# A two-layer decoder: head scores from spread keys in 32-row tiles instead of from zero-padded keys by head

## What is computed

```python
Q, K, V = (a.reshape(B, S, 16, 8).transpose(0, 2, 1, 3) for a in (x @ wq.T, c @ wk.T, c @ wv.T))
score = jnp.einsum('bhqd,bhkd->bhqk', Q, K) / jnp.sqrt(8)
attn  = jax.nn.softmax(score, axis=-1)
out   = jnp.einsum('bhqk,bhkd->bhqd', attn, V).transpose(0, 2, 1, 3).reshape(B, S, 128)
```

## Time and profile before

| | |
|---|---|
| median of 3 runs | 496.33 us (494.31 to 496.59) |
| span of the profiled execution | 492.2 us |
| TensorE busy | 420.9 us, 86% |
| TensorE weight loads | 340.0 us, 69% |
| VectorE busy | 311.8 us, 63% |
| ScalarE busy | 235.1 us, 48% |
| GpSimd busy | 48.6 us, 10% |

### The profile page before, as it was taken

How to read it: one execution, slowest core, us unless ns; L and a number is a source line. 1 busy time by engine, 2 the same in 40 slices (tenths; PEclk the granted TensorE clock), 3 DMA queues, 4 the chain that set the end, 5 groups by cost and what they waited for, 6 DMA issues and landing times.

```text
span 492.2 us, 9126 instructions
## 1 busy us (share of the span) xinstructions
PE 420.9 (86%) x3332; PEld 340.0 (69%) x3332; DVE 311.8 (63%) x916; ACT 235.1 (48%) x527; POOL 48.6 (10%) x56
## 2 busy tenths in 40 slices
PE   3589898999999978998798989999999969984393
PEld 2476666668999966675766766668999956652292
DVE  3686766673555678685867667754755577763534
ACT  2147656663334326654255757572433437571131
POOL 6200282000000000002020000000000000010114
PEclk9889999999999999999789999999999989998588
DMA  8403323600010010002010201000010042060301
GB/s 282 142 25 89 78 72 96 161 1 1 2 31 14 2 43 1 1 3 53 1 37 16 45 1 43 1 1 2 1 43 3 1 132 82 1 182 1 95 7 34
DMA packets 18906, 22.52 MB, mean 46 GB/s; under 512 B 2984, under 2 KB 13361, under 8 KB 18864
## 3 DMA queue, kind: packets, MB, share of 16 engines
q1 hardware_dynamic: 17344, 18.68, 14.3%
q10 hardware_dynamic: 1008, 2.31, 1.4%
q0 software_dynamic: 512, 0.97, 0.6%
HBM read 13.63 MB, written 2.11 MB: 32 GB/s over the span
## 4 chain that ended last, share of the span: by engine, by line
PE 64%; DVE 21%; ACT 7%; issue 4%; DMA 1%; SPq 0%; POOLq 0%; POOL 0%; DVEq 0%; ACTq 0%
PE bank_C L809 12%; PE bank_S L675 8%; PE bank_C L703 7%; PE bank_E L687 7%; DVE negmax L1171 5%; PE bank_M L609 3%; ACT expo L953 2%; PE bank_M L738 2%; PE bank_M L611 2%; PE bank_E L797 2%; PE bank_S L797 2%; PE bank_M L661 2%; PE bank_E L799 2%; PE bank_E L798 2%; DVE x_rows L1219 1%
## 5 line engine op out<-in xcount | busy, mean ns | idle before, releaser
L1171 DVE TENSOR_REDUCE negmax<-bank_S 128x2 f32<-128x512 f32 x192 | 128.4, 685 | 50.3 <-PE bank_S L675 50.1
L953 ACT ACTIVATE expo<-bank_E 128x512 f32<-128x512 f32 x192 | 113.5, 597 | 83.5 <-PE bank_E L687 82.3
L675 PE MATMUL bank_S<-k_head,q_sp 128*128 128x256 f32 x384 | 97.0, 338 | 10.7 <-DVE negmax L1171 7.2
L675 PEld LDWEIGHTS bank_S<-k_head,q_sp 128*128 128x128 f32 x384 | 61.5, 199 | 39.1 <-issue 25.0
L687 PE MATMUL bank_E<-q_sh,k_head 128*128 128x256 f32 x384 | 81.3, 294 | 0.7 <-DVE q_sh L1166 0.5
L703 PE MATMUL bank_C<-expo,v_aug 128*32 128x256 f32 x768 | 61.5, 393 | 4.6 <-ACT expo L953 4.6
L687 PEld LDWEIGHTS bank_E<-q_sh,k_head 128*128 128x128 f32 x384 | 60.3, 194 | 6.5 <-issue 3.5
L809 PE MATMUL bank_C<-mix_w,expo 128*128 128x128 f32 x512 | 62.5, 275 | 0.7 <-issue 0.7
L809 PEld LDWEIGHTS bank_C<-mix_w,expo 128*128 128x128 f32 x512 | 59.9, 192 | 1.1 <-issue 1.1
L1014 ACT ACTIVATE expo<-bank_S,b 128x256 f32<-128x256 f32 x64 | 26.8, 470 | 53.6 <-PE bank_S L799 53.2
L1276 DVE TENSOR_SCALAR expo<-bank_E,b 128x256 f32<-128x256 f32 x64 | 27.9, 477 | 28.1 <-PE bank_E L799 28.0
(11 more groups left out here) (185 smaller groups left out, 654.7 us busy)
## 6 DMA issues: line engine op xcount, KB each, us to landing
k_head<-expo SPq DMA_DIRECT2D x96, 64.0 KB, 2.0
mix_w<-in_mix_w SPq DMA_DIRECT2D x24, 256.0 KB, 3.3
expo<-in_mix_w SPq DMA_DIRECT2D x6, 256.0 KB, 6.1
proj_w<-in_proj ACTq DMA_DIRECT2D x1, 640.0 KB, 11.5
xe_scratch<-empty_row SPq DMA_DIRECT2D x1, 520.0 KB, 6.1
expo<-xe_scratch SPq DMA_DIRECT2D x2, 260.0 KB, 3.1
expo<-in_spread SPq DMA_DIRECT2D x1, 512.0 KB, 7.9
expo<-in_spread ACTq DMA_DIRECT2D x1, 512.0 KB, 8.5
```

Of the source, the lines that this page charges most:

```text
L675: last = mm(where(seq, b, ("max", k))[:, qt * SEQ:(qt + 1) * SEQ], q_sp[seq][:, t, qt * P:(qt + 1) * P], k_head[seq][:, t, g, :], start=Tr ...
L953: activate(expo[seq][:, h % ESLOTS, :], where(seq, b, ("exp", h))[:], ACT.Exp, scale=scale).then_inc(free(seq, b, ("exp", h)), 1)
L1171: V.tensor_reduce(negmax[seq][:, k // 4, :, 32 * (k % 4)], where(seq, b, ("max", k))[:].rearrange("p (q n) -> p q n", q=QT), AX.X, ALU.max ...
```

## The change

Keys are no longer laid out by head. `k_sp` becomes a tensor of its own, and both score products take the 32 rows of the head's group from the spread tensors directly: a matmul of 32 rows by 128 columns, at row 0, 32, 64 or 96. In a step that has both kinds, the four matmuls alternate: first half of head k's scores, first half of head k - 7's, then the second halves. Head k lies in row group k mod 4, head k - 7 in the next one. `k_head`, its DMAs, its zeroing and its semaphores are gone; step 0 waits for ScalarE's emptying of the key spread instead. GpSimd's memsets of `v_aug[1]` and `negmax[1]` move to the first block, in place of the first memset of `k_head`.

```diff
-        k_head = lanes("k_head", [P, GROUPS, 4, SEQ], f32r)
+        k_sp = lanes("k_sp", [P, GROUPS, SEQ], f32r)
...
-        k_sp = [e[:, ESLOTS - 2:ESLOTS, :].rearrange("p a (t n) -> p (a t) n", n=SEQ).bitcast(f32r)
-                for e in expo]
...
             @block.gpsimd
             def _(pool):
-                nc.gpsimd.memset(k_head[0][:].bitcast(u32), 0)
+                nc.gpsimd.memset(v_aug[1][:].bitcast(u32), 0).then_inc(v1_zeroed, 1)
+                nc.gpsimd.memset(negmax[1][:].bitcast(u32), 0)
...
-                nc.gpsimd.memset(v_aug[1][:].bitcast(u32), 0).then_inc(v_zeroed, 1)
-                nc.gpsimd.memset(negmax[1][:].bitcast(u32), 0)
-                nc.gpsimd.memset(k_head[1][:].bitcast(u32), 0)
-                pool.wait_ge(v_zeroed, 2)
+                pool.wait_ge(v1_zeroed, 1)
...
-                def by_head(seq, b, what):
...
-                    wait_drained(sp, seq, b, what)
-                    if seq == 1:
-                        sp.wait_ge(lane1_zeroed, 1)
-                    t = slice(2 * half, 2 * half + 2)
-                    for g in range(4):
-                        r = slice(32 * g, 32 * g + 32)
-                        sp.dma_start(k_head[seq][r, t, g, :].bitcast(f32),
-                                     k_sp[seq][r, t, :].bitcast(f32)
-                                     ).then_inc(k_head_ready[seq][half], 16)
...
+                def score(seq, b, h, qt):
+
+                    t, g = h // 4, slice(32 * (h % 4), 32 * (h % 4) + 32)
+                    return mm(where(seq, b, ("max", h))[:, qt * SEQ:(qt + 1) * SEQ],
+                              q_sp[seq][g, t, qt * P:(qt + 1) * P], k_sp[seq][g, t, :],
+                              start=True, stop=True)
+
+                def shifted_score(seq, b, h, kt):
+
+                    t, g = h // 4, slice(32 * (h % 4), 32 * (h % 4) + 32)
+                    return mm(where(seq, b, ("exp", h))[:, kt * SEQ:(kt + 1) * SEQ],
+                              k_sp[seq][g, t, kt * P:(kt + 1) * P], q_sh[seq][g, t, :],
+                              start=True, stop=True)
...
                             if k == 0:
                                 wait_drained(pe, seq, b, "sq0")
-                                pe.wait_ge(k_head_ready[seq][0], 64 * (MHA[b] + 1))
+                                wait_drained(pe, seq, b, "sk0")
...
-                            for qt in range(QT):
-                                last = mm(where(seq, b, ("max", k))[:, qt * SEQ:(qt + 1) * SEQ],
-                                          q_sp[seq][:, t, qt * P:(qt + 1) * P],
-                                          k_head[seq][:, t, g, :],
-                                          start=True, stop=True)
-                            last.then_inc(full(seq, b, ("max", k)), 1)
...
-                            for kt in range(QT):
-                                last = mm(where(seq, b, ("exp", h))[:, kt * SEQ:(kt + 1) * SEQ],
-                                          k_head[seq][:, t, g, kt * P:(kt + 1) * P],
-                                          q_sh[seq][:, t, :],
-                                          start=True, stop=True)
-                            last.then_inc(full(seq, b, ("exp", h)), 1)
+                        for half in range(2):
+                            if k < HEADS:
+                                last = score(seq, b, k, half)
+                                if half == 1:
+                                    last.then_inc(full(seq, b, ("max", k)), 1)
+                            if 0 <= k - EXP_AT < HEADS:
+                                h = k - EXP_AT
+                                last = shifted_score(seq, b, h, half)
+                                if half == 1:
+                                    last.then_inc(full(seq, b, ("exp", h)), 1)
```

More of the change, by code:

```diff
@@ L369, in decoder @@
         spread_k_ready, spread_q_ready = sem("spread_k_ready"), sem("spread_q_ready")
-        v_zeroed, lane1_zeroed = sem("v_zeroed"), sem("lane1_zeroed")
+        v_zeroed, v1_zeroed, lane1_zeroed = sem("v_zeroed"), sem("v1_zeroed"), sem("lane1_zeroed")
         empty_row_ready, slots_emptied = sem("empty_row_ready"), sem("slots_emptied")
@@ L375, in decoder @@
         drained = {pool: [sem(f"drained_{pool}{i}") for i in range(n)] for pool, n in POOLS.items()}
-        k_head_ready = [[sem(f"k_head_ready{i}_{half}") for half in range(2)] for i in range(BATCH)]
         split_q_ready = [sem(f"split_q_ready{i}") for i in range(BATCH)]
@@ L533, in _ @@
             def _(sp):
-                def by_head(seq, b, what):
-                    half = int(what[2])
-                    wait_drained(sp, seq, b, what)
-                    if seq == 1:
-                        sp.wait_ge(lane1_zeroed, 1)
-                    t = slice(2 * half, 2 * half + 2)
-                    for g in range(4):
-                        r = slice(32 * g, 32 * g + 32)
-                        sp.dma_start(k_head[seq][r, t, g, :].bitcast(f32),
-                                     k_sp[seq][r, t, :].bitcast(f32)
-                                     ).then_inc(k_head_ready[seq][half], 16)
                 def load(place, name, e, loaded):
@@ L550, in _ @@
                 for seq, b, what in TURNS:
-                    if what in ("sk0", "sk1"):
-                        by_head(seq, b, what)
-                    elif b == SELF0 and seq < LANES and what[0] == "pv":
+                    if b == SELF0 and seq < LANES and what[0] == "pv":
                         wait_filled(sp, seq, b, what)
@@ L665, in heads @@
                         if k < HEADS:
-                            t, g = k // 4, k % 4
                             if k == 0:
                                 wait_drained(pe, seq, b, "sq0")
-                                pe.wait_ge(k_head_ready[seq][0], 64 * (MHA[b] + 1))
+                                wait_drained(pe, seq, b, "sk0")
                             if k == 8:
                                 wait_drained(pe, seq, b, "sq1")
-                                pe.wait_ge(k_head_ready[seq][1], 64 * (MHA[b] + 1))
+                                wait_drained(pe, seq, b, "sk1")
@@ L681, in heads @@
                             h = k - EXP_AT
-                            t, g = h // 4, h % 4
-                            if g == 0:
-                                wait_drained(pe, seq, b, ("shift", t))
+                            if h % 4 == 0:
+                                wait_drained(pe, seq, b, ("shift", h // 4))
                             wait_free(pe, seq, b, ("exp", h))
-                            for kt in range(QT):
-                                last = mm(where(seq, b, ("exp", h))[:, kt * SEQ:(kt + 1) * SEQ],
-                                          k_head[seq][:, t, g, kt * P:(kt + 1) * P],
-                                          q_sh[seq][:, t, :],
-                                          start=True, stop=True)
```

## The result

The changed kernel takes 583.84 us (577.74 to 590.38, four runs) against 495.94 us of the kernel before beside it: a ratio of 1.169, interval 1.164 to 1.174. The prediction said 496.8 and a range of 486 to 510. The profiled execution has a span of 575.5 us, 83.3 more than the 492.2 of before.

The account below looks back on a forecast made before the run. Bound: fixed-length chains through VectorE and ScalarE inside head-pass stretches. Start -3.7 and -0.5, stretches -0.2, mixture +3.8, seq 2 +1.2 and -0.8, slow stretch +0.3, ends +0.4 sum to +0.5 on 496.33: 496.8 us, range 486 to 510.

Parts of the forecast that it names:

- rival 4: Head steps: the clock drops as fewer rows work, giving 550 us; chance 0.04.
- (f): Output product to transpose of x: VectorE filled without a gap, so fixed at 3.86 us; change 0.
- Rival 1: Steps with both kinds: loads or matmuls of two row groups don't overlap, giving 510 us; chance 0.22.
- (a): Scores 0 to 2 of a stretch: next shifted score waits for a shift behind one VectorE row maximum; fixed, 0.
- (b): From there to the values: two switches round the shift and three coincidences, less 0.33 us of waiting; +0.06 us.
- (c): Values to the back transposes: exp 7 is full sooner, ScalarE does exponential and copy; -0.23 us.
- (d): k projection to key spread: TensorE's 0.84 us idle hides two switches; 0, or +0.16 without that cover.
- (e): Key spread to the output product: two switches and a pair; +0.16 us.
- (g): Step 14 and the queries: -0.04 us, and -0.12 because the exponential ahead of the evacuation is earlier.
- (h): Query spread to exp 16: one switch; +0.20 us.
- Rival 2: Switches between 32-row tiles and whole array are cheaper: 480 us at no cost, 488 at half; chance 0.27.
- rival 3: Slices run as whole-array instructions with idle rows, so neither pairs nor switches, giving 491 us; chance 0.05.

Follow-up runs that it names:

- the early-start kernel: Kernel before, second lane's key memset moved and sequence 0's first four row maxima taken as 32-row tiles from the spread keys: 490.7 us, ratio 0.987 to 0.992.
- the small kernel: Separate kernel of only f32r matmuls of 256 columns, in stretches behind 110 whole-array ones; one 32-row group alone fell to 1.2 GHz, 0.21 us a matmul.
- the experiment with tiles between values: Kernel with memset moved and early first score, plus 32-row tiles for six of 32 score products per head pass, between column tiles: 491.7 us against 490.7.

## Why the prediction was wrong

**The step that failed** is rival 4 and what it stood for: the sum took the clock of each stretch over from before. I gave a drop 0.04 and sized it at a third of each stretch's TensorE work (+56 us, 550). It is what happened, and larger: 250 us more at 1.2 GHz, about half the head passes wholly, +82 us by the estimate above. The trace of before held a warning that I read too lightly: its clock was 0.62 from 236 to 247 (rows 5), far from the start, and it fell in head steps behind waits of 1.20 and 0.77 us (TensorE in order of time, then the stretches on either side of the fall, in the columns of rows 5):

```profile
236.77 0.50 PE L675 MATMUL bank_S<-k_head,q_sp 128*128 128x256 f32 x2 [1.20 <-DVE negmax L1171]
238.04 0.44 PE L749 MATMUL bank_M<-const,x_rows 128*128 128x128 f32 x2 [0.77 <-DVE x_rows L1219]
236.00:238.60 2.60, 0.94 (x4) 0.50 (x4) 2.47 (x10) 0.58 (x3) 0.00 (x0) 1.00 0.00 0
238.80:247.00 8.20, 8.03 (x35) 7.76 (x35) 6.28 (x26) 2.59 (x6) 0.56 (x1) 0.50 0.01 2
```

So the clock of the head steps could not be taken as given; what the trace couldn't say is that idle rows count, which no row of before showed.

Once the clock is down, "fixed" stops being fixed. Piece (f), 3.86 to 3.89 us of VectorE's work at the full clock in both kernels, takes 5.96 at the lower one: in the same order VectorE waits for TensorE.

**The rest, step by step, at the full clock.**

TensorE at the full clock after; the line of before that answers to the four matmuls in a row is 79.65 to 80.31, 0.67 us (rows 6).

```profile
45.05 0.64 PE L692 MATMUL bank_C<-expo,v_aug 128*32 128x256 f32 x8 [0.24 <-ACT expo L942]
45.62 0.38 PE L635 MATMUL bank_S<-k_sp,q_sp 32*128 32x256 f32 x1
45.62 0.38 PE L642 MATMUL bank_E<-q_sh,k_sp 32*128 32x256 f32 x1
45.84 0.27 PE L635 MATMUL bank_S<-k_sp,q_sp 32*128 32x256 f32 x1
45.84 0.28 PE L642 MATMUL bank_E<-q_sh,k_sp 32*128 32x256 f32 x1
46.05 0.64 PE L692 MATMUL bank_C<-expo,v_aug 128*32 128x256 f32 x8
```

- *Start*: 16.06 predicted as 16.0, the first cast 0.29 us. Right, and shown by the early-start kernel to reach the end. The memset's share was -1.4 predicted, -1.8 measured (interval -0.9 to -2.4). The -0.5 for a clock that rises earlier went the other way in the changed kernel: its clock stood at 0.50 from 18.0 to 31.6, where before it had 0.52 from 20 to 26.5 only. Seq 2's -0.8 can't be read, as its stretch runs at the lower clock.
- *Pairs*: two tiles of different row groups start within 0.01 us of each other, 0.43 us for the step instead of 0.67, the -0.23 predicted. Rival 1 is out: the loads of different row groups lie beside each other. The Trainium skill, in "TensorE: Matmul & The Clock Gate", part on packing small matmuls, gives about 4 ns from tile to tile, and the trace agrees. Its rule on loads that overlap only across row groups doesn't hold for whole-array loads here (rows 4), nor for 32-row tiles of one group (26 matmuls and 26 loads in 3.00 us, in the small kernel).
- *Switch*: mis-sized. Two changes round a shift (38.98, 39.41, 39.78 after) take 0.32 us more than before, three round the key spread from 186.59 to 188.59 take 0.48: 0.16 each, not 0.195. Beside column tiles the row tiles cost the same as the whole array, as my sum had it: from the values' start to the next scores 0.57 us in both kernels (rows 6, and 45.05 to 45.62 above), from a lone shifted score to the values 0.40 in both (65.39 to 65.79 before, 41.05 to 41.45 after; the first line below is of before, the other two of after). So between two runs of values a step with both kinds gains by its pairs and pays for no change more; the experiment with tiles between values rests on that.

```profile
65.79 0.64 PE L703 MATMUL bank_C<-expo,v_aug 128*32 128x256 f32 x8
41.05 0.47 PE L642 MATMUL bank_E<-q_sh,k_sp 32*128 32x256 f32 x2 [0.30 <-ACT expo L942]
41.45 0.64 PE L692 MATMUL bank_C<-expo,v_aug 128*32 128x256 f32 x8
```

- *(a)*: not fixed. From score 0 to the first shifted score of the next four heads 1.75 became 2.07 (38.98 to 41.05): the two switches round the shift delay the shifted scores behind it, and by ScalarE's exponentials the next ones.
- *(b)*, with (a): +0.06 predicted, -0.01 to -0.03 measured (6.08 and 6.10 to 6.07); the pairs between the values pay for the shift. *(c)* -0.23, measured -0.25. *(d)* and *(e)* 0 and +0.16, measured together 0 (5.88 both). *(f)* 0 and 0. *(g) and (h)*: -0.16 and +0.20, measured together +0.10 (81.85 to 87.02 before, 86.13 to 91.40 after). The pieces met at full clock add up to -0.18 for a stretch with key spread, against +0.03.
- *Mixture*: from the lone score at 174.99 to the causal block's product behind the transpose +0.86 measured (7.96 before, 8.81 after, from 186.59). The mark lies behind the first of the four switches; without it the forecast is 0.885 (0.78 - 0.195 + 0.3), so this was right.

So the working inside a stretch was right to a few tenths of a us, in part by errors that cancel: (a) and the cheaper switch. At an unchanged clock the kernel would by these pieces have come out some 2 to 4 us on the fast side; that is an estimate that no run shows. Rival 2 pointed the right way (0.16 instead of 0.195, not half), rival 3 is out (tiles start side by side).

**What is not settled.** That the loss comes by the clock is shown, and that idle rows alone can bring it down too. In the decoder changes of tiling bring it down as well, and how much of the 250 us falls to either is open: the kernel with row maxima alone in 32 rows fits neither theory. Why its runs can settle at 0.79 or 0.90 these runs don't tell.

## What to carry to other kernels

A product in 32 of 128 rows without partners in the other row groups takes as long as a whole-array one (0.12 us for 256 columns) and can cost the clock of all that runs beside it. Multiplying zeros isn't wasted where it keeps TensorE at 2.4 GHz, so fill all four row groups or keep the padded form. Never take the clock of a stretch as given when the rows in use change. Take a change apart before judging it: here the early start was worth 4 to 6 us by itself, and was hidden under 88 us of loss.

## What the runs showed of the hardware that I had not expected

- An unbroken stream of f32r matmuls in one 32-row group goes from 2.4 to 1.2 GHz (from 0.12 to 0.21 us each), and one over two row groups in turn doesn't. The Trainium skill ("TensorE: Matmul & The Clock Gate", section on oscillation) describes losses of the clock by waits between bursts; this stream has no waits and loses it all the same.
- 384 added whole-array matmuls made a kernel 8 to 13 us faster (ratios 1.169 to 1.153, medians 583.8 to 570.5).
- A change between row tiles and the whole array costs 0.16 us at the full clock; one between row and column tiles costs the same as one between whole array and column tiles (0.57 us from the values to the next scores and 0.40 from a lone shifted score to the values, with either).
- GpSimd's memset of 3.5 us made a VectorE cast beside it 1.675 instead of 0.29 us long; moving it gave 1.8 us of the total.
